# Self attention's scores and masks as tiles of 32 rows by 64 columns, from two copies of the keys

## The reference, cut to what matters

```python
q = (x @ wq).reshape(b, s, 32, 16); k = (x @ wk).reshape(b, s, 8, 16); v = (x @ wv).reshape(b, s, 8, 16)
scores = einsum('bihd,bjhd->bhij', q, repeat(k, 4)) * 16 ** -0.5
scores = where(causal, scores, finfo.min)
x = x + einsum('bhij,bjhd->bihd', softmax(scores), repeat(v, 4)) @ wo
```

## Time and profile before

| | |
|---|---|
| median of 3 runs | 1612.97 us (1612.93 to 1615.87) |
| profiled execution | 1612.89 us, its span 1611.2 us |
| mean granted TensorE clock | 0.999 of its full speed |
| PE, DVE, ACT, POOL busy | 98%, 70%, 46%, 39% of the span |
| self attention's loops | about 49.6 to 133.6 us of the span in the first half, and the same stage near 845 to 930 us in the second |

### The profile page before, as it was taken

One profiled execution on the slowest core, in us unless ns is written; L12 is line 12 of the kernel. 1 busy time (PEld: TensorE's weight loads), 2 busy tenths in 40 slices (PEclk: granted clock), 3 DMA queues, 4 the chain that ended last, 5 costly groups with the idle time before them and its releaser, 6 DMA issues.

```text
span 1611.2 us, 40988 instructions
## 1 busy us (share of the span) xinstructions
PE 1583.7 (98%) x16856; PEld 1319.8 (82%) x16856; DVE 1122.8 (70%) x1983; ACT 747.2 (46%) x1402; POOL 635.8 (39%) x531
## 2 busy tenths in 40 slices
PE   7999999999999999999999999999999999999998
PEld 6667888888888888789886688888888888887997
DVE  6696867677576676885657968667676676668744
ACT  4674545435355354431247744535444444544321
POOL 5693433424243242551228824424243342434501
PEclk9999999999999999999999999999999999999999
DMA  6000201102020120131220002112020120201100
GB/s 227 27 28 8 67 8 59 44 21 65 0 65 20 46 72 0 45 108 52 67 79 27 21 1 68 33 33 65 0 65 20 46 60 5 72 8 60 46 14 27
DMA packets 26285, 71.57 MB, mean 44 GB/s; under 512 B 3168, under 2 KB 3424, under 8 KB 26208
## 3 DMA queue, kind: packets, MB, share of 16 engines
q1 hardware_dynamic: 26208, 70.48, 14.2%
HBM read 66.27 MB, written 4.19 MB: 44 GB/s over the span
## 4 chain that ended last, share of the span: by engine, by line
PE 84%; DVE 8%; POOL 3%; ACT 2%; issue 2%; DMA 0%; SPq 0%; POOLq 0%; DVEq 0%; ACTq 0%
PE acc L441 14%; PE acc L442 13%; PE acc L443 13%; PE y L441 10%; PE y L442 10%; PE y L443 10%; PE quad L756 6%; PE quad L785 4%; PE y L769 2%; DVE psum_ L1536 1%; POOL prob L1897 1%; PE acc L459 1%; POOL prob L1903 1%; PE quad L441 1%; DVE pmax L1531 1%
## 5 line engine op out<-in xcount | busy, mean ns | idle before, releaser
L1876 POOL TENSOR_TENSOR qkrs<-qkve,mhalf 128x10 f32<-128x10 f32 x64 | 125.1, 1954 | 307.9 <-DVE qkve L1501 307.9
L441 PE MATMUL y<-w_hi 128*128 128x512 f32 x576 | 228.3, 396 | 3.3 <-DVE x L1543 2.5
L443 PE MATMUL y<-w_hi,w_lo 128*128 128x512 f32 x576 | 224.4, 390 | 0.0
L442 PE MATMUL y<-w_lo,w_hi 128*128 128x512 f32 x576 | 224.4, 390 | 0.0
L441 PE MATMUL acc<-w_hi,xn_hi 128*128 128x512 f32 x512 | 207.0, 404 | 0.0
L442 PE MATMUL acc<-w_lo,xn_hi 128*128 128x512 f32 x512 | 201.2, 393 | 0.0
L443 PE MATMUL acc<-w_hi,xn_lo 128*128 128x512 f32 x512 | 199.5, 390 | 0.0
L1406 DVE TENSOR_TENSOR x<-y,x 128x512 f32<-128x512 f32 x128 | 88.3, 690 | 140.1 <-PE y L443 140.1
L1859 POOL TENSOR_TENSOR w_lo<-stage,w_hi 128x1024 fp32r<-128x1024 f32 (+1 forms) x80 | 156.6, 1966 | 61.9 <-ACT w_hi L945 57.9
L1495 DVE TENSOR_REDUCE qkss<-kspace 128x4 f32<-128x512 f32 x128 | 87.4, 682 | 108.2 <-ACT kspace L984 107.6
L441 PE MATMUL acc<-w_hi,cx_hi 128*128 128x256 f32 x512 | 149.7, 292 | 1.7 <-DVE xn_lo L1330 1.7
(11 more groups left out here) (161 smaller groups left out, 3919.8 us busy)
## 6 DMA issues: line engine op xcount, KB each, us to landing
stage<-in_w_cross SPq DMA_DIRECT2D x64, 512.0 KB, 3.6
stage<-in_w_cross SPq DMA_DIRECT2D x32, 256.0 KB, 2.7
stage<-in_w_ffn SPq DMA_DIRECT2D x16, 512.0 KB, 3.6
stage<-in_w_self SPq DMA_DIRECT2D x8, 512.0 KB, 6.2
out_x<-x SPq DMA_DIRECT2D x16, 256.0 KB, 2.0
x<-in_x SPq DMA_DIRECT2D x6, 512.0 KB, 5.6
kt<-in_ctx SPq DMA_DIRECT2D x8, 256.0 KB, 4.0
prob<-in_ctx SPq DMA_DIRECT2D x8, 256.0 KB, 4.2
```

Of the source, the lines that this page charges most:

```text
L441: nc.tensor.matmul(target, l_hi, r_hi, start=first, stop=False)
L442: nc.tensor.matmul(target, l_hi, r_lo, start=False, stop=False)
L443: return nc.tensor.matmul(target, l_lo, r_hi, start=False, stop=last)
L1876: return nc.gpsimd.tensor_tensor(target, source, mhalf[:, 0:width], ALU.pow)
```

## The change

- Keys: `kt` gets a sibling. DVE writes two copies of the keys (`kk`, by `keys_out`), one with the odd heads' rows zeroed and one with the even heads' (`parity`), four tensor_scalar operations of 128x512 in each half. ACT's `keys_out` and DVE's `spread_keys` (16 in each half) are gone.
- Scores: for each unit 8 matmuls of 32 rows (two key heads) by 64 columns (two query heads), each row group into a bank of its own. The moving side has 64 columns (near) or 128 (far). Then 8 bf16 matmuls of the same tiling add the mask (64 columns each). Near and far lie side by side in the 4 banks of `quad`, and both are complete before ACT copies either.
- Banks: transposed probabilities now have one bank (`acc[0]`) in place of two, the output `acc[1]`, and the last queries and the norm's transposes one of their own (`solo`, `y[1]`).
- Order: on all engines the two units of one sequence now go through the softmax in one step of the loop. PE transposes the two units with a half of the step's projection or query work between them (`behind`), and the norm's steps lie one step later. The lists of ACT, DVE and POOL follow. Two pieces of weights (512 columns each) are split by DVE instead of POOL (`weights_lo`), so POOL has 8 strips (p = 5 to 12) instead of 12.
- End of the stage: `second_norm(5)` stands ahead of the first query projection of cross attention instead of behind it, `second_norm(6)` ahead of the second key projection.

```diff
-        sc = [quad[:, 0, 0:256].rearrange("p (g k) -> p g k", g=NG), quad[:, 1].rearrange("p (g k) -> p g k", g=NG)]
-        pt = [quad[:, 3], y[1]]
-        ot1 = quad[:, 2]
+        near = quad[:, :, 0:SEQ].rearrange("p i (g k) -> p i g k", g=2)
+        far = quad[:, :, SEQ:3 * SEQ].rearrange("p i (g k) -> p i g k", g=2)
+        pt1, ot1, solo = acc[0][:], acc[1][:], y[1][:]
...
             def transpose_probs(at, u, buffer):
-                if u == 0:
-                    pe.wait_ge(y_free.sem, at(y_free, 0))
-                    pe.wait_ge(ot_lo_done.sem, at(ot_lo_done, 0))
-                    pe.wait_ge(gaps_clear.sem, at(gaps_clear, 1))
                 pe.wait_ge(s_nrm.sem, at(s_nrm, u + 1))
-                pe.wait_ge(pt_done.sem, at(pt_done, max(u - 1, 0)))
-                to = pt[u % 2]
+                pe.wait_ge(pt_done.sem, at(pt_done, u))
                 for k in range(4):
-                    ins = nc.tensor.transpose(to[:, k * P:(k + 1) * P], prob[:, buffer, k * P:(k + 1) * P], ident[:])
+                    ins = nc.tensor.transpose(pt1[:, k * P:(k + 1) * P], prob[:, buffer, k * P:(k + 1) * P], ident[:])
                 ins.then_inc(pt_rdy.sem, 1)
...
                     if b == 0:
                         pe.wait_ge(proj_out.sem, at(proj_out, 8))
+                        evacuated(pe, at, A1[half]["kt0"])
                     if b == NSEQ // 2:
-                        for n in range(REP, 2 * REP):
+                        evacuated(pe, at, A1[half]["kt1"])
+                        for n in (4, 5):
                             evacuated(pe, at, A1[half][f"q{n}"])
-                    pe.wait_ge(kbd_done.sem, at(kbd_done, b + 1))
-                    near, far = (slice(l * SEQ // 2, (l + 1) * SEQ // 2) for l in range(2))
-                    queries = [q1t[:, b, l].rearrange("p r q -> p (r q)") for l in range(2)]
-                    pe.wait_ge(s_add.sem, at(s_add, max(2 * b - 1, 0)))
-                    nc.tensor.matmul(sc[0], queries[0], kbd[:, b % 2, :, near], start=True, stop=False)
-                    nc.tensor.matmul(sc[0], ident_b[:], causal_b[:], start=False, stop=True).then_inc(sc_rdy.sem, 1)
+                        pe.wait_ge(solo_free.sem, at(solo_free, 2))
                     pe.wait_ge(s_add.sem, at(s_add, 2 * b))
-                    nc.tensor.matmul(sc[1], queries[1], kbd[:, b % 2], start=True, stop=False)
-                    nc.tensor.matmul(sc[1][:, :, far], ident_b[:], causal_b[:], start=False, stop=True
-                                     ).then_inc(sc_rdy.sem, 1)
+                    for l, scores in enumerate((near, far)):
+                        keys = slice(b * SEQ, b * SEQ + (l + 1) * SEQ // 2)
+                        halves = [(i, h, slice(32 * i, 32 * (i + 1))) for i in range(4) for h in range(2)]
+                        for i, h, rows in halves:
+                            nc.tensor.matmul(scores[h * SEQ:(h + 1) * SEQ, i],
+                                             q1t[rows, b, l, 2 * h:2 * h + 2].rearrange("p r q -> p (r q)"),
+                                             kk[rows, :, keys], start=True, stop=False)
+                        for i, h, rows in halves:
+                            ins = nc.tensor.matmul(scores[h * SEQ:(h + 1) * SEQ, i, :, l * SEQ // 2:],
+                                                   query_b[rows, 2 * h:2 * h + 2].rearrange("p r q -> p (r q)"),
+                                                   causal_b[rows], start=False, stop=True)
+                        ins.then_inc(sc_rdy.sem, 1)
...
+                def behind(p, second):
+                    if p == 0:
+                        for k in ((2,) if second else (0, 1)):
+                            self_query_part(half, 6, k)
+                    elif p == 1:
+                        if not second:
+                            self_query_part(half, 6, 3)
+                    elif p < 4:
+                        self_query_part(half, 7, 2 * (p - 2) + second)
+                    else:
+                        if p == 4 and not second:
+                            pieces_split(place, 5)
+                        i = (p - 4) // 2
+                        project_part(at, i, i + 1, 2 * (p % 2) + second, y[0], i)
+                pe.wait_ge(y_free.sem, at(y_free, 0))
+                pe.wait_ge(gaps_clear.sem, at(gaps_clear, 1))
                 for p in range(NSEQ + 1):
                     if p + AHEAD < NSEQ:
                         scores1(p + AHEAD)
-                    if p == 0:
-                        query_parts(0)
                     if p >= 1:
                         values1(2 * p - 2)
                         values1(2 * p - 1)
+                    if p == 0:
+                        behind(0, 0)
+                        evacuated(pe, at, A1[half]["kt1"])
                     if p < NSEQ:
                         transpose_probs(at, 2 * p, (2 * p) % URING)
+                    if p > 0:
+                        behind(p, 0)
+                    else:
+                        behind(0, 1)
+                    if p < NSEQ:
                         transpose_probs(at, 2 * p + 1, (2 * p + 1) % URING)
-                    if 0 < p < 4:
-                        query_parts(p)
-                    if p == 4:
-                        pieces_split(place, 5)
-                    if p >= 4:
-                        i = (p - 4) // 2
-                        for h in (2 * (p % 2), 2 * (p % 2) + 1):
-                            project_part(at, i, i + 1, h, self_y(i), i)
-                    if p >= 8 and p % 2 == 0:
-                        second_norm((p - 8) // 2)
+                    if p > 0:
+                        behind(p, 1)
+                    if p >= 9 and p % 2 == 1:
+                        second_norm((p - 9) // 2)
                 for h in (2, 3):
-                    project_part(at, 6, 7, h, self_y(6), 6)
+                    project_part(at, 6, 7, h, y[0], 6)
+                second_norm(4)
                 first = Place(2, half, 0)
                 project_chunk_kv(first, 0)
...
+                second_norm(5)
+                pe.wait_ge(ot_lo_done.sem, at(ot_lo_done, NT))
+                normed(1)
                 project_chunk_q(first, 0)
-                second_norm(5)
                 second_norm(6)
                 project_chunk_kv(first, 1)
+                normed(3)
                 project_chunk_q(first, 1)
...
                 def copy_scores(u):
-                    act.wait_ge(sc_rdy.sem, at(sc_rdy, u + 1))
-                    nc.scalar.copy(seen(u, u % URING), sc[u % 2]).then_inc(s_add.sem, 1)
+                    act.wait_ge(sc_rdy.sem, at(sc_rdy, u // 2 * 2 + 2))
+                    target = seen(u, u % URING).rearrange("p (i g) k -> p i g k", i=4)
+                    nc.scalar.copy(target, far if u % 2 else near).then_inc(s_add.sem, 1)
...
                 for p in range(-AHEAD, NSEQ + 1):
                     scored = p + AHEAD < NSEQ
...
                         self_queries(half, 5)
                     if scored:
                         copy_scores(2 * (p + AHEAD))
-                    if 0 <= p + 1 < NSEQ:
-                        unit_exps(at, 2 * (p + 1) + 1)
+                        copy_scores(2 * (p + AHEAD) + 1)
+                    if 0 <= p < NSEQ:
+                        evacuate_probs(at, 2 * p, 0)
                     if scored:
-                        copy_scores(2 * (p + AHEAD) + 1)
                         unit_exps(at, 2 * (p + AHEAD))
                     if p >= 2 and p % 2 == 0:
                         i = (p - 2) // 2
                         act.wait_ge(pv_done.sem, at(pv_done, 4 * i + 4))
                         output_hi(i)
                     if 0 <= p < NSEQ:
-                        evacuate_probs(at, 2 * p, 0)
                         evacuate_probs(at, 2 * p + 1, 1)
+                    if scored:
+                        unit_exps(at, 2 * (p + AHEAD) + 1)
                     if p in (1, 3):
                         self_queries(half, 6 + p // 2)
-                    if p >= 8 and p % 2 == 0:
-                        second_norm_hi((p - 8) // 2)
+                    if p >= 9 and p % 2 == 1:
+                        second_norm_hi((p - 9) // 2)
                     if 0 <= p < NSEQ - 2:
                         spread_values(p + 2)
-                    if p in (1, 3, 5, 9):
-                        n = (1, 3, 5, 9).index(p)
+                    if p in (0, 2, 4, 7):
+                        n = (0, 2, 4, 7).index(p)
                         if n > 1:
-                            act.wait_ge(acc_rdy.sem, at(acc_rdy, A1[half]["q7"] + 1))
+                            act.wait_ge(solo_rdy.sem, at(solo_rdy, 2))
                         else:
                             act.wait_ge(proj_rdy.sem, at(proj_rdy, 8))
                         split_piece(Place(2, half, 0), n)
...
             def self_attention(half):
                 at = Place(1, half).at
-                def spread_keys(b):
```

(103 more changed lines are left out.)

56 lines of the change are left out of this document (34 added, 22 removed).

## The result

The changed kernel takes 1630.54 us (median; 1629.69 to 1632.22) against 1612.97 in the same series: 1.0104 of before, 95% interval 1.0089 to 1.0119. A second series on another chip gave 1.0099 (1.0082 to 1.0116). It is slower by 17.6 us. I had forecast slower, but by 3, and the time lies above the range.

A forecast was written before the change was run, and what follows sets the result against it. PE was full before; the softmax's serial chain was to set the changed loop's pace. Cross attention 3.3 us later, less 1.7 in the tail, net 1.6 per half, 3.3 for two: 1612.9 + 3.3 gives 1616 us, own range 1611 to 1621, overall 1604 to 1627.

The forecast's parts named there:

- Scores: PE, one sequence's scores and masks: 0.95 us instead of 1.61, with 0.2 for entering and leaving the tiling.
- Rival C: PE's scores: small matmuls don't overlap, over 1.8 us a sequence, PE the bound again; 1635 or 1658 us; chance 0.10.
- The serial chain: Softmax in the loop: the path through one far unit sets the step, 4.32 us, or 5.01 with a strip.
- Rival A: Loop: the engines' sums decide, about 4.05 us a step instead of 4.93, 13 us a half; 1587 us; chance 0.15.
- What the new order costs: Loop: term that adds the softmax's chain and collisions; last far multiplication ends at 126.1, with collisions at 129.6.
- PE's 3.84 or 4.27: Loop: PE's work per step in us, the larger with the norm's transposes, said to lie under the 4.32 chain.
- the sum of collisions: Loop, per half: output_hi 1.7, weights_lo 0.9, the norm's operation and the 1024-column split 0.9; together 3.5 us.
- After the loop: Cross attention's first projection starts 7.3 us after the last multiplication, at 136.9 instead of 133.57, 3.3 later.
- The clock: PE's granted clock stays at 1.00 in the stage; falling with 10 to 15% idle would make the prediction too low.
- The tail's gain: End of the stage: second_norm(5) and (6) no longer wait 0.83 and 0.87 us; 1.7 us saved per half.
- D: One bank of transposed probabilities: evacuations in series with transposes lose 0.3 us more a step; 1626 us; chance 0.20.
- B: Loop: the chain without collisions, 3.5 us less per half, net -1.9 a half; 1609 us; chance 0.20.

The follow-up runs named there:

- e6_double_scores: e2_add_and_stats with every score and mask matmul issued twice, same output: 1622.27 us, 1.0045 of before.
- e7_keep_clock: The changed kernel with 14 throwaway transposes in each of PE's steps 8, 10, 12 and 14: 1627.25 us, 1.0078 of before.
- e1_add_first: The changed kernel with DVE's addition to x ahead of the two maxima, as before the change: 1623.66 us, 1.0065 of before.
- e2_add_and_stats: e1_add_first with the norm's statistics also ahead of the sums in odd steps: 1619.59 us, 1.0037 of before.
- e4_interleave_and_add: The changed kernel with DVE's addition ahead of the maxima and the softmax's order of before on ACT, DVE and POOL: 1609.71 us, 0.9978 of before.
- e5_before_add_late: The kernel before with one edit, DVE's addition to x behind the two maxima: 1625.64 us, 1.0072 of before.

## Why the prediction went wrong

**Scores: right, a little too dear.** One sequence's scores and masks run from 85.19 to 85.97, 0.78 us in the changed kernel, against 0.95 predicted and 1.61 before. Near scores take 16 records, the far ones 16, the masks 16. The term that was too dear is the 0.2 for entering and leaving the tiling: without it the sum was 0.76. Rival C is out. The first scores, and the first operation behind the masks:

```profile
85.19 0.37 PE L654 MATMUL quad<-kk,qb 32*64 32x64 f32 x16
...
85.97 0.65 PE L676 MATMUL acc<-probt,vbd 128*32 128x128 f32 x16
```

**The serial chain: right.** 4.32 without a strip appears to the hundredth (60.28 to 64.60), 5.01 with one in step 7 (93.92 to 98.93). The forecast that almost all that the engines saved would be lost in it holds: e6_double_scores shows that the pace doesn't depend on PE. Rival A is out. A `weights_lo` stretched a POOL multiplication to 1.39 us instead of 1.04, `output_hi` added 0.27 to an even step (step 2, 69.27 to 73.86, is 4.59): against 0.45 and 0.28 as put. Rival A's own sum was off as well: 14 steps by 0.88 and the tail's 1.7 are 14 us a half, not 13, which gives 1585 and not 1587.

**The step that failed** is in "What the new order costs": "PE's 3.84 or 4.27 lie under it, and so do DVE's operations", and with it the sum of collisions, 3.5 us. I had checked busy time, and that each operation was ready for POOL. I had not followed what waits for DVE's addition, though the diff shows it moved: PE's projection, and behind that on PE the second transposes, on ACT their evacuation and the far exponential. For the even steps the path to add up was the far sum, statistics, two maxima, addition, three products, transposes, evacuation, exponential: about 6.4 us at the full clock, by my estimate from the rows of steps 9 and 10, and not 5.29. e7_keep_clock, with the wait and without the slow clock, shows 6.31 to 6.53 for these steps. Measured from the first to the last subtraction are 78.9 us against 73.8. e1_add_first and e2_add_and_stats shorten this path and reach 75.0 and 73.7. Together they give back 0.0067 of the 0.0104, 0.0039 by the addition alone.

**After the loop,** the term was 7.3 us from the last multiplication to cross attention's first projection. It measured 10.05 (134.82 to 144.87). PE waits for the addition in step 14 too, 2.19 us, where the term had no wait. No maxima stand in this step; the addition comes behind the far sum and the norm's statistics of step 13. With the statistics earlier (e2_add_and_stats) the wait is 1.33:

```profile
135.41 0.47 PE L429 MATMUL y<-w_hi 128*128 128x512 f32 x1 [2.19 <-DVE x L1575]
...
144.87 0.36 PE L429 MATMUL acc<-w_hi,cx_hi 128*128 128x256 f32 x1
```

**The clock** was forecast to stay at 1.00. That it might fall "with 10 to 15% idle in short gaps" was named as a sign of a prediction that is too low, without a price. It did fall, behind waits of up to 3.32 us. By e7_keep_clock that was some 3 us of the 17 for the run.

**The tail's gain** was 2.1 us a half instead of 1.7: from cross attention's first projection to the scores at 184.19 before were 50.62 us, in the changed kernel 48.53 (144.87 to 193.40):

```profile
193.40 1.59 PE L782 MATMUL quad<-kk,qb 32*64 32x64 f32 x128
```

**Sum for the first half:** loop 134.82 instead of 129.6 (5.2), wait and more behind it (2.7), tail (-0.4): 7.5 over the predicted 1.6, 9.2 in the trace. The span grew by 16.8 us in all, so the second half lost somewhat less, 7.6; its subtractions lie 77.3 us apart (856.63 to 933.94).

**The rivals.** D came near in time (1626), but its mechanism was the evacuation in series with the transposes. What is late in the changed kernel is the addition, and PE's order, with products between the two transposes of a step, passes the delay on to the far exponential. What the one bank costs was not tested by a run with two. It isn't nothing: in e4_interleave_and_add PE waits 14 times, 10.6 us in all up to 140 us, for ACT's copy out of that bank. B's figure, 1609, lies near e4_interleave_and_add, which reached it by another order. What e2_add_and_stats still lacks to the predicted 1616, 3 us, lies behind the loop: its first projection of cross attention starts 9.0 us behind the last multiplication (129.74 to 138.78), not 7.3, with the wait of 1.33 in it. With the first subtraction 0.25 later than put (51.65) and the tail 0.4 better, that is about 1.6 a half, and 3 for two if the second half is like the first.

## What to carry to other kernels

When an operation moves within an in-order list, follow both directions: what it now waits for, and who waits for it and what is queued behind that one on its engine, until the path closes or ends. A list that looks harmless by busy time can close a ring across four engines. Cheap work on a full engine pays only when the order of the others lets it run at its new pace: doubling the scores cost 1 us under the serial softmax and 11 us under the interleaved one. Free a shared buffer before the steps that wait for later work.

## What the runs showed of the hardware

An idle stretch of 3.32 us on PE was followed by 3.6 us at a granted clock of 0.52, one of 1.49 us was not. But the length of the last wait doesn't decide it alone. In the changed kernel PE's products came slowly at once behind a wait of only 1.68 us (0.53 and 0.43 us apart instead of 0.31 and 0.23), and behind one of 2.32 us only after 1.1 us of work at the full clock:

```profile
112.40 0.47 PE L429 MATMUL y<-w_hi 128*128 128x512 f32 x1 [2.32 <-DVE x L1575]
...
113.93 0.63 PE L430 MATMUL y<-w_lo,w_hi 128*128 128x512 f32 x1
...
123.93 0.74 PE L429 MATMUL y<-w_hi 128*128 128x512 f32 x1 [1.68 <-DVE x L1575]
124.46 0.63 PE L430 MATMUL y<-w_lo,w_hi 128*128 128x512 f32 x1
```

Behind the 2.19 us of step 14, and behind the 2.48 us in e5_before_add_late, the clock stayed at 1.00. In e2_add_and_stats it was 0.84 from 100 to 110 us, though no wait of PE from 90 us on was longer than 1.33:

```profile
90.00:100.00 10.00, 7.52 (x131) 5.07 (x122) 6.85 (x19) 7.63 (x19) 7.56 (x11) 0.99 0.01 2
100.00:110.00 10.00, 9.86 (x161) 6.84 (x161) 7.41 (x19) 7.09 (x17) 8.03 (x12) 0.84 0.17 54
```

What decides it stays open here. The 14 transposes a step of e7_keep_clock, whose results nobody reads, were enough to keep the clock at 1.00.

Small tiled matmuls overlapped as well as in the scores of cross attention: 48 records in 0.78 us with the switching of the tiling in it, though a third of them are bf16 behind f32 into the same banks. At 11.9 ns for 64 columns, the rate of the earlier trace rows, they would be 0.76.
